# Experts work on gathered tokens in four column groups, with weights loaded by a number found on the chip

## The chip, the cores and the metric

The kernel runs on one core of one Trainium2 chip, alone. The time is device microseconds for one execution. The engines are TensorE (PE; its weight load is PEld), VectorE (DVE), ScalarE (ACT), GpSimd (POOL), and SyncE (SP), whose queue here only issues DMAs. DMAs are issued by SP, ACT and POOL queues.

## The reference, cut to what matters

The model is a stack of twelve layers on x, of 2 batches of 128 tokens of 256 numbers, all in float32. The change is in the third: a mixture of experts with two shared blocks and sixteen routed experts. Each token chooses two experts.

```
shared_out = _gated_mlp(x, shared_w1, shared_w3, shared_w2)      # silu(x @ w1.T) * (x @ w3.T) @ w2.T, 512 wide
gates = softmax(x @ wg.T)                                        # 16 experts
topk_w, topk_idx = top_k(gates, 2);  topk_w /= sum(topk_w)
combine = zeros(T, 16).at[rows, topk_idx].set(topk_w)            # T = 256 tokens
for each expert (w1, w3, w2, cw):                                # 256 wide
    acc = acc + cw[:, None] * _gated_mlp(x, w1, w3, w2)
out = shared_out + acc
```

Ahead of it stand a cross attention on a context of 2 x 2048 tokens and an mLSTM with a gated MLP of four blocks. Behind it comes a causal-style cross attention on the same context (32 units of head and batch).

## The kernel before, in words

Every engine has one program, written out in order; semaphores order the engines among each other. Nothing is planned at run time.

**Gated blocks.** The MLP (blocks 0 to 3), the shared expert (4 and 5) and the sixteen experts (6 to 21) are 22 blocks of one shape: 256 wide up parts w1 and w3, and a down part w2, 768 KB for the three. `Gated.up` (L460) makes eight products of 128 x 128 weights with all 256 tokens; L422 is their line. ACT takes silu of one half (L489), DVE multiplies by the other (L496), `Gated.down` (L470) makes four products (L480), and DVE adds the result to x, for the experts scaled by the token's weight for this expert (L508, L510). So each expert computes all 256 tokens, and the weight is zero for those that didn't choose it. PE issues the up part of block n+1 ahead of the down part of block n. Weights lie in a ring of three slots in the tile `big`; SP loads block n+3 when block n's down part is done (L458). The experts run in a loop of three blocks a turn. The last block's adds are `add_last` (L562), called from the stage behind, which starts with them.

**Router.** `Router.vector` (L788) finds the two largest logits of a token with small DVE operations on 32 columns; it runs beside block 4's up part.

**Around it.** `Split` (L1367) turns the context's keys into three bfloat16 parts, 16 blocks of four POOL operations and a store to DRAM (`key_parts`): six ahead of the mLSTM, ten after block 4's gate. `Mlstm` (L565) needs POOL three times for a root (L152, L153), at the start, in the middle and near the end. `Early` (L1046) computes keys and values for a later layer in 16 pieces, in the gaps of PE; its keys (L1089) are products with 32 stationary columns in four column groups of the array, its values are L1097. SP stores its pieces (L1118). `Causal` (L1463) is the stage behind: SP loads the split keys of unit u in three DMAs (L1422) into one of four slots in the tile `kt`, four units ahead, and one piece of 256 KB of later weights a unit (L1561). PE makes the scores (L1582) and transposed scores (L1593), DVE the maxima (L1716), POOL a shift (L1517), ACT the exponentials (L1663), PE the product with the values in the tile `vv` (L1434). The values were loaded at the start for the first cross attention and stay. POOL's `gpsimd` (L1503) of it begins with a memset of three partitions of `kt` (L1508) and, once the last block is down, a mask (L1510).

## Time and profile before

| | us |
|---|---|
| median of 3 runs | 1100.19 |
| lowest, highest | 1099.86, 1101.62 |
| the profiled execution | 1103.23 |
| its span | 1101.4 |
| gated blocks 4 to 21 in it | 146.3 to 241.8 |

The granted clock of PE was 0.993 over the span. PE ran 9611 products and as many weight loads, of 23433 instructions in all. The core moved 100.39 MB, a mean of 91 GB/s. In the page's 40 slices (27.5 us each) the DMA engines were busiest in the first two (383 and 299 GB/s). A row of a stretch gives busy us of each engine with the number of its operations, the granted clock (1.00 is 2.4 GHz, 0.50 is 1.2 GHz), the DMA engines' busy share and GB/s. In the chain a row is a piece of the work that ended last.

### The profile page before, as it was taken

The page shows a single profiled execution, that of the slowest core. Times are in us where ns is not written, and L with a number is a line of the kernel's source. Part 1 is how long each engine was busy: PE and PEld are TensorE (multiplying, and loading weights), DVE is VectorE, ACT ScalarE, POOL GpSimd, SP SyncE. Part 2 cuts the span into 40 slices and gives each one's busy share as a digit, 9 for nine tenths or more (in the row PEclk, how much of TensorE's full clock was granted, in tenths as well). Part 3 has the DMA queues.
Part 4 walks back from the last instruction along what each step waited for, and adds up shares of the span by engine and source line. Part 5 has one row for each costly group of instructions (what it writes and reads, how often), then busy time and mean ns, then how long its engine had stood idle before and what let it go on. Part 6 is the DMA issues. An engine that isn't in the chain of part 4 may idle for free.

```text
span 1101.4 us, 23433 instructions
## 1 busy us (share of the span) xinstructions
PE 1041.8 (95%) x9611; PEld 845.6 (77%) x9611; DVE 698.0 (63%) x1330; ACT 504.3 (46%) x876; POOL 234.0 (21%) x360
## 2 busy tenths in 40 slices
PE   8999999998999989999988899999999999999886
PEld 3765778875777646677775788999999999999764
DVE  3655243247788368888744876776666577677466
ACT  3242232126677448888855624433342233332384
POOL 4701048402132000000010711110001043332120
PEclk9999999999999999999999999999999999999997
DMA  9712346554673517000141000131111122100000
GB/s 383 299 69 79 133 164 214 191 148 121 184 193 106 178 41 263 2 2 2 40 153 40 1 1 20 33 120 41 39 39 58 40 77 68 59 20 10 1 1 10
DMA packets 37158, 100.39 MB, mean 91 GB/s; under 512 B 4033, under 2 KB 12609, under 8 KB 35393
## 3 DMA queue, kind: packets, MB, share of 16 engines
q1 hardware_dynamic: 33152, 87.35, 24.2%
q0 software_dynamic: 2752, 9.44, 2.5%
q10 hardware_dynamic: 1152, 2.16, 0.5%
q8 instruction: 74, 1.21, 0.5%
q14 instruction: 28, 0.22, 0.1%
HBM read 83.73 MB, written 15.20 MB: 90 GB/s over the span
## 4 chain that ended last, share of the span: by engine, by line
PE 81%; DVE 12%; ACT 3%; issue 2%; DMA 1%; POOL 1%; SPq 0%; DVEq 0%; ACTq 0%; POOLq 0%
PE ps L2276 11%; PE ps L2233 10%; PE ps L422 8%; PE ps L1434 6%; PE ps L1790 6%; PE ps L2131 4%; PE ps L2120 4%; PE ps L480 3%; PE ps L1781 3%; PE ps L1582 3%; PE ps L1593 3%; PE ps L415 3%; PE ps L1097 2%; PE ps L1089 2%; PE ps L291 1%
## 5 line engine op out<-in xcount | busy, mean ns | idle before, releaser
L2276 PE MATMUL ps<-vv,prob 128*128 128x129 f32 x1024 | 126.5, 276 | 1.7 <-DVE xn L2463 1.7
L2276 PEld LDWEIGHTS ps<-vv,prob 128*128 128x128 f32 x1024 | 119.6, 191 | 2.5 <-ACT prob L2382 2.1
L2415 DVE TENSOR_REDUCE probT<-ps 128x128 f32<-128x1024 f32 x64 | 82.5, 1290 | 21.9 <-PE ps L2233 12.9
L1716 DVE TENSOR_REDUCE st<-ps 128x1 f32<-128x512 f32 x128 | 82.4, 686 | 18.0 <-PE ps L1582 16.0
L2382 ACT ACTIVATE prob<-prob 128x1024 f32<-128x1024 f32 x64 | 71.1, 1111 | 27.4 <-DVE prob L2427 27.4
L2355 ACT COPY w<-ps 128x128 f32<-128x128 f32 x32 | 8.5, 266 | 160.0 <-PE ps L2242 160.0
L422 PE MATMUL ps<-xT,big 128*128 128x256 f32 x352 | 79.8, 381 | 0.7 <-ACT xT L707 0.7
L2427 DVE TENSOR_TENSOR prob<-ps,probT 128x1024 f32<-128x1024 f32 x64 | 79.6, 1285 | 1.1
L1663 ACT ACTIVATE prob<-ps 128x1024 f32<-128x1024 f32 x64 | 65.8, 1030 | 28.0 <-PE ps L1593 26.8
L422 PEld LDWEIGHTS ps<-xT,big 128*128 128x128 f32 x352 | 66.2, 190 | 11.2 <-ACT xT L707 0.9
L152 POOL TENSOR_SCALAR small<-small 128x4 f32<-128x4 f32 (+1 forms) x44 | 9.9, 226 | 300.3 <-DVE small L2170 156.3
L2233 PE MATMUL ps<-big,kt 128*128 128x128 f32 x512 | 60.2, 276 | 2.3 <-DVE prob L2427 2.3
L2233 PEld LDWEIGHTS ps<-big,kt 128*128 128x128 f32 x512 | 58.5, 192 | 3.8 <-DVE prob L2427 2.2
L2233 PE MATMUL ps<-w,kt 128*128 128x128 f32 x512 | 60.0, 275 | 0.0
L2233 PEld LDWEIGHTS ps<-w,kt 128*128 128x128 f32 x512 | 58.4, 192 | 0.1
L496 DVE TENSOR_TENSOR prob<-prob,ps 128x512 f32<-128x512 f32 x22 | 15.1, 687 | 67.0 <-ACT prob L489 67.0
L1845 ACT COPY big<-ps 128x512 f32<-128x512 f32 x80 | 45.4, 588 | 20.1 <-PE ps L1790 20.1
L2163 ACT ACTIVATE kt<-ps,w 128x512 f32<-128x512 f32 x32 | 21.8, 690 | 71.4 <-PE ps L2140 71.4
L489 ACT ACTIVATE prob<-ps 128x512 f32<-128x512 f32 x22 | 13.1, 597 | 86.3 <-PE ps L422 86.3
L153 POOL TENSOR_TENSOR small<-small,const 128x4 f32<-128x4 f32 (+1 forms) x44 | 51.0, 1158 | 3.7
L2120 PE MATMUL ps<-qz,big 128*128 128x128 f32 x384 | 47.1, 276 | 0.7 <-ACT kt L2163 0.7
L2131 PE MATMUL ps<-qz,big 128*128 128x128 f32 x384 | 47.0, 275 | 0.0
(476 smaller groups left out, 2282.6 us busy)
## 6 DMA issues: line engine op xcount, KB each, us to landing
big<-blocks_in SPq DMA_DIRECT2D x22, 768.0 KB, 4.3
big<-ctxT_in SPq DMA_DIRECT2D x24, 512.0 KB, 4.1
key_parts<-w POOLq DMA_DIRECT2D x16, 384.0 KB, 4.7
kt<-key_parts SPq DMA_DIRECT2D x32, 192.0 KB, 3.3
vv<-ctx_in SPq DMA_DIRECT2D x2, 2176.0 KB, 24.9
vv<-early_values SPq DMA_DIRECT2D x4, 1088.0 KB, 12.0
kt<-ctxT_in SPq DMA_DIRECT2D x2, 2048.0 KB, 12.4
kt<-key_parts SPq DMA_DIRECT2D x32, 128.0 KB, 3.2
```

The lines of the kernel that those rows point to most:

```text
L422: last = pe.matmul(out, w[:, c, lo:lo + P], xT[:, :, c, :], start=(c == 0), stop=(c == DC - 1))
L1434: last = pe.matmul(self.k.ps[g:g + 17, bank, 0:P], self.values(u, ch), pT[:, ch * P:(ch + 1) * P], start=(ch < 4), stop=(ch + 4 >= MC))
L1663: act.activation(self.pT[:, u % 2, h * 1024:(h + 1) * 1024], k.bank(2 + 2 * h, 1024, 2), ACT.Exp).then_inc(s("exp"), 1)
L1716: dve.tensor_reduce(self.mx[:, u % 2, n:n + 1], k.ps[:, n % 2, :], AX.X, ALU.max).then_inc(s("reduced"), 1)
L1790: last = pe.transpose(k.ps[:, bank, ch * P:(ch + 1) * P], self.p[u % 4][:, (4 * n + ch) * P:(4 * n + ch + 1) * P], k.const("ident"))
L2120: last = pe.matmul(k.ps[:, bank, t * P:(t + 1) * P], tile[:, c, t * P:(t + 1) * P], self.ctx("wk_ctx", DC)[:, c, h * DH:(h + 1) * DH], sta ...
L2131: last = pe.matmul(k.ps[:, bank, t * P:(t + 1) * P], tile[:, c, t * P:(t + 1) * P], self.ctx("wv_ctx", DC)[:, c, h * DH:(h + 1) * DH], sta ...
L2233: last = pe.matmul(k.ps[:, ch // 4, ch % 4 * P:ch % 4 * P + P], keys[:, ch * P:(ch + 1) * P], q, start=True, stop=True)
L2276: last = pe.matmul(k.ps[:, 7, 0:DH + 1], self.prob(u)[:, ch * P:ch * P + P], v, start=(ch == 0), stop=(ch == MC))
L2382: act.activation(e, e, ACT.Exp).then_inc(s("c3_exp"), 1)
L2415: dve.tensor_reduce(self.largest[:, h * P:(h + 1) * P], bank.rearrange("p (c t) -> p t c", t=P), AX.X, ALU.max).then_inc(s("c3_max"), 1)
L2427: dve.tensor_tensor(self.prob(u)[:, lo:hi].rearrange("p (c t) -> p c t", t=P), k.bank(0, hi, 5)[:, lo:hi].rearrange("p (c t) -> p c t", t= ...
```

## The change

Each expert now computes only tokens that chose it. The 512 choices (256 tokens, two each) get places in 32 blocks of 32 slots. Blocks 0 to 15 are the first 32 choices of expert 0 to 15. What an expert has above 32 goes to further blocks, 16 to 31, which are given out in order of the experts. A round works on four blocks at once, one in each column group; there are 8 rounds. The weights of blocks 0 to 15 are loaded by number into sixteen homes. After round t's up and down parts, its homes are loaded with the weights of blocks 16 + 4t to 19 + 4t: SP reads the expert's number from SBUF into a register and issues a DMA at a computed address, once for the up parts (512 KB) and once for the down part (256 KB).

- PE: `ranks` counts choices ahead of a token with products of triangular and all-ones matrices; `rows` turns eight columns (places and weights) into rows; `gather` multiplies the normalized tokens by a one-hot matrix (256 tokens by 128 slots), so that each column group has its 32 tokens as stationary columns; `up` streams 512 columns of w1 and w3 through them; `turn` transposes the gated result; `down` streams 256 columns; `combine` multiplies by a weighted one-hot matrix and accumulates in the two PSUM banks that already hold the shared experts' sum. x is added to once, at the end.
- DVE: `tables` and `places` (16 small operations) and, per round, `make_pick`, `gate`, `make_give`. ACT: per round four operations of 256 columns.
- The four MLP blocks and the two shared ones stay as they were, with a ring at another place of `big`. The tiles w03, kt, vv, big, prob and qz become parts of one arena, so that homes lie in any of them. Expert 0 to 3 take most of `vv`, whose values are loaded again for the stage behind, in four DMAs of 1.04 MB.
- POOL: the split blocks move: 6 to 14 stand between the mLSTM's first and second root, 15 between the second and third. The memset of `kt` is cut in two; its second half runs when the experts are done.
- SP: experts 0 to 9 are loaded ahead of the MLP, 10 to 15 during blocks 3 to 5, the found ones in the rounds. Keys of units 0 and 1 are loaded ahead of the found weights, those of 2 and 3 behind the last combine.

The semaphores of the mLSTM are renamed (m_ to l0_) and used on. The diff, cut to its core:

```diff
+HOMES = [begin("vv") + MC * VH * q for q in range(4)] + [begin("w03"), begin("qz") + 512]
+HOMES += [begin("big") + EXP * i for i in range(3)] + [begin("kt") + 2048]
+HOMES += [begin("big") + EXP * i for i in (5, 3, 4, 6, 7)] + [begin("prob")]
...
+    LOADED = (80, 80, 48, 96, 96, 64)       # Gated.up(n) waits for block_in{n % 3}
...
+class Experts:
+    def load_found(self, sp, dram, t, lo, n, sem):
+        for g in range(4):
+            i = 4 * t + g
+            e = sp.value_load(self.found[0:1, i:i + 1], min_val=0, max_val=EXPERTS - 1)
+            at = HOMES[i] + lo
+            sp.dma_start(self.k.arena[:, at:at + n], dram[bass.ds(e, 1)].rearrange("a p n -> (a p) n")[:, lo:lo + n]).then_inc(self.k.s(sem), 16)
+    def found_sync(self, sp, dram):
+        sp.wait_ge(s("l0_hin"), 4)
+        for t in range(5):
+            if t < 4:
+                sp.wait_ge(s("block_up"), 6 + t + 1)
+                if t >= 2:
+                    sp.wait_ge(*((s("w0_in"), 96) if t % 2 else (s("block_in1"), 160)))
+                self.load_found(sp, dram, t, 0, 1024, "w0_in" if t % 2 else "block_in1")
+            if t >= 1:
+                sp.wait_ge(s("block_y"), 6 + t)
+                if t >= 2:
+                    sp.wait_ge(s("block_in2"), 64 + 64 * (t - 1))
+                self.load_found(sp, dram, t - 1, 1024, 512, "block_in2")
+    def early_sync(self, sp, dram, moe, early):
+        ...                                  # stores 0, 1
+        sp.wait_ge(s("c_product"), 8)
+        for e in range(4):
+            self.load(sp, dram, e, "block_in0")
+        early.store(sp, 2)
+        sp.wait_ge(s("l0_proj"), 3)
+        self.load(sp, dram, 4, "block_in1")
+        for n in range(3, 10):
+            early.store(sp, n)
+        sp.wait_ge(s("l0_hin"), 2)
+        ...                                  # experts 5 to 7 (block_in1), 8 and 9 (block_in2), store 10, tables
+    def up(self, pe, t):
+        ...
+        for c in range(DC):
+            for g in range(4):
+                last = pe.matmul(k.ps[32 * g:32 * g + 32, t % 2, :], self.tokens[t % 2][:, c * P + 32 * g:c * P + 32 * g + 32],
+                                 self.weight(t, g, 512 * c, 512), start=(c == 0), stop=(c == 1))
+    def down(self, pe, t):
+        ...                                  # the same with hT and 256 columns, into bank 4
+    def gather(self, pe, t):
+        ...
+        for c in range(DC):
+            for b in range(B):
+                last = pe.matmul(k.ps[:, 2 + t % 2 * 3, c * P:(c + 1) * P], k.xn[:, b, c * P:(c + 1) * P], self.pick[t % 2][:, b * P:(b + 1) * P],
+                                 start=(b == 0), stop=(b == 1))
+    def combine(self, pe, t):
+        ...
+        for b in range(B):
+            last = pe.matmul(k.ps[:, 6 + b, b * D:(b + 1) * D], self.give[t % 2][:, b * P:(b + 1) * P], self.y[t % 2],
+                             start=False, stop=(t == ROUNDS - 1))
+    def tensor(self, pe):
+        gated.up(pe, 4)
+        self.ranks(pe)
+        gated.up(pe, 5)
+        gated.down(pe, 4)
+        gated.down(pe, 5)
+        self.rows(pe)
+        self.gather(pe, 0)
+        self.gather(pe, 1)
+        for t in range(ROUNDS + 3):
+            if t < ROUNDS:
+                self.up(pe, t)
+            if 0 <= t - 2 < ROUNDS:
+                self.down(pe, t - 2)
+            if 0 <= t - 1 < ROUNDS:
+                self.turn(pe, t - 1)
+            if 0 <= t - 3 < ROUNDS:
+                self.combine(pe, t - 3)
+            if t + 2 < ROUNDS:
+                self.gather(pe, t + 2)
+    def vector(self, dve, o, between):
+        self.gated.gate(dve, 4)
+        self.tables(dve, o)
+        self.gated.gate(dve, 5)
+        self.make_pick(dve, o, 0)
+        self.make_pick(dve, o, 1)
+        self.places(dve, o)
+        ...                                  # per round: make_pick(t + 2), gate(t), make_give(t - 1)
...
 class Causal: sync
         for u in range(32):
             if u >= 4:
                 sp.wait_ge(*self.at("keys_queries", 2 * (u - 3)))
+            if u == 2:
+                found_sync()
+                sp.wait_ge(k.s("l0_proj"), 6 + ROUNDS)
             self.load_keys(sp, u)
-            if u == 3:
-                early.stored(sp, early.LATE)
-                sp.wait_ge(k.s("block_y"), 23)
+            if u in (2, 3, 4, 5):
+                self.reload_values(sp, u - 2, ctx)
...
 build: gpsimd
-            Mlstm.gpsimd(k, pool, o)
+            Mlstm.gpsimd(k, pool, o, 0, 1)
+            split.gpsimd(pool, o, split.BEFORE_MLSTM, split.LAST)
+            Mlstm.gpsimd(k, pool, o, 1, 2)
+            split.gpsimd(pool, o, split.LAST, len(split.BLOCKS))
+            Mlstm.gpsimd(k, pool, o, 2, 3)
             Norm.gpsimd(k, pool, o, 2)
-            pool.wait_ge(s("block_h"), 5)
-            split.gpsimd(pool, o, split.BEFORE_MLSTM, len(split.BLOCKS))
```

## Rows read from the trace of the kernel before

**Rows 1.** The page's parts 1 and 4, of the whole span

```profile
PE 1041.8 (95%) x9611; PEld 845.6 (77%) x9611; DVE 698.0 (63%) x1330; ACT 504.3 (46%) x876; POOL 234.0 (21%) x360
...
PE 81%; DVE 12%; ACT 3%; issue 2%; DMA 1%; POOL 1%; SPq 0%; DVEq 0%; ACTq 0%; POOLq 0%
```

**Rows 2.** Stretches: window and us, busy us by engine, granted clock, DMA share, GB/s

```profile
10.00:20.00 10.00, 8.87 (x32) 3.38 (x32) 5.61 (x9) 3.90 (x4) 8.26 (x8) 1.00 1.03 433
...
146.30:241.80 95.50, 95.03 (x438) 81.86 (x438) 32.50 (x79) 20.71 (x28) 46.89 (x52) 1.00 0.57 184
...
258.00:268.00 10.00, 9.78 (x174) 6.98 (x172) 7.99 (x16) 7.57 (x14) 3.38 (x12) 1.00 0.70 198
...
274.00:276.00 2.00, 2.00 (x23) 1.05 (x25) 1.48 (x3) 1.02 (x1) 0.00 (x0) 0.50 0.19 29
```

**Rows 3.** Chain in order of time: start us, us, what

```profile
69.21 1.88 PE ps L742 x16
...
98.24 0.87 PE ps L755 x8
...
140.29 1.85 PE ps L1089 x16
...
145.35 1.06 PE ps L415 x8
146.41 7.00 PE ps L422 x32
153.42 1.73 PE ps L480 x8
155.14 3.45 PE ps L422 x16
...
241.01 0.50 DVE x L562
```

**Rows 4.** Timeline, ACT and DVE: start us, us, engine line op, idle before

```profile
60.99 0.38 ACT L680 COPY attT<-ps 128x256 f32<-128x256 f32 x1 [2.08 <-PE ps L422]
...
85.70 0.42 DVE L641 TENSOR_TENSOR big<-att 128x256 f32<-128x256 f32 x1
...
149.71 0.19 DVE L813 TENSOR_TENSOR small<-small 128x32 f32<-128x32 f32 x1
...
152.05 0.69 DVE L496 TENSOR_TENSOR prob<-prob,ps 128x512 f32<-128x512 f32 x1
```

**Rows 5.** DMA issues, 140 to 245 us: size, median us from issue to landing

```profile
big<-blocks_in SPq DMA_DIRECT2D x16, 768.0 KB, 4.3
...
early_keys<-big ACTq DMA_DIRECT2D x1, 256.0 KB, 2.1
```

**Rows 6.** Timeline of 225 to 275 us, SP's queue

```profile
228.62 0.33 SPq L458 DMA_DIRECT2D big<-blocks_in  x1
229.22 8.22 SPq L1422 DMA_DIRECT2D kt<-key_parts  x12
```

**Rows 7.** Timeline of POOL, around the mLSTM and beside the experts

```profile
54.66 0.69 POOL L153 TENSOR_TENSOR st<-st,const 128x2 f32<-128x2 f32 x1
103.46 0.21 POOL L152 TENSOR_SCALAR small<-small 128x16 f32<-128x16 f32 x1 [48.10 <-DVEq L643]
...
177.13 0.62 POOL L1387 CAST w<-kt 128x512 bf16<-128x512 f32 x1
...
182.01 0.61 POOL L1387 CAST w<-kt 128x512 bf16<-128x512 f32 x1
...
202.04 3.51 POOL L1508 MEMSET kt<- 3x4096 f32 x1
```

**Rows 8.** Timeline of the stage behind the experts: POOL, SP's queue, PE

```profile
250.89 0.19 POOL L1517 CAST probT<-st 128x1 bf16<-128x1 f32 x1 [8.32 <-DVE st L1727]
...
258.65 3.05 SPq L1422 DMA_DIRECT2D kt<-key_parts  x3
...
271.52 0.59 PE L1582 MATMUL ps<-kt,qz 96*128 96x512 bf16 x2 [1.45 <-issue]
```

More of the change, by code:

```diff
@@ L523, in mlp_vector @@
             if n < 4:
-                self.gate(dve, n, n % 3)
+                self.gate(dve, n)
             if n >= 1:
-                self.add(dve, n - 1, (n - 1) % 3)
-    def moe(self, eng, first, second):
-        first(4, 1, 1)
-        with eng.Fori(0, self.TIMES) as i:
-            for j in range(3):
-                n = i * 3 + (4 + j)
-                first(n + 1, (2 + j) % 3, i + (5 + j) // 3)
-                second(n, (1 + j) % 3, i * 3 + j)
-        for n in range(4 + 3 * self.TIMES, self.LAST):
-            if n + 1 < self.LAST:
-                first(n + 1, (n + 1) % 3, (n + 1) // 3)
-            second(n, n % 3, n - 4)
@@ L543, in moe_tensor @@
-    def moe_tensor(self, pe):
-        self.moe(pe, lambda n, r, t: self.up(pe, n, r, t), lambda n, r, m: self.down(pe, n, r))
-    def moe_scalar(self, act):
-        with act.Fori(0, BLOCKS_MOE // 3) as i:
-            for j in range(3):
-                self.silu(act, i * 3 + (4 + j), (1 + j) % 3)
-    def moe_vector(self, dve):
-        cw = self.k.cw
-        def second(n, r, m):
-            if not isinstance(n, int) or n < self.LAST - 1:
-                self.add(dve, n, r, lambda b: cw[:, bass.ds(m + b * BLOCKS_MOE, 1)])
-        self.moe(dve, lambda n, r, t: self.gate(dve, n, r), second)
+                self.add(dve, n - 1)
@@ L661, in vector, with gpsimd @@
             last = dve.scalar_tensor_tensor(t[:, b], k.xn[:, b], k.st[:, 38 + b:39 + b], w("norm2_w"), ALU.mult, ALU.mult)
-        last.then_inc(s("m_hin"), 1)
+        last.then_inc(s("l0_hin"), 1)
     @staticmethod
-    def gpsimd(k, pool, o):
+    def gpsimd(k, pool, o, first, last):
         s = k.s
-        for n in range(3):
+        for n in range(first, last):
             pool.wait_ge(s("sum_squares"), n + 1)
@@ L791, in v @@
             return k.small[:, 160 + 32 * i:192 + 32 * i].rearrange("p (b e) -> p b e", b=B)
-        lg, key, pick, sel, e = v(0), v(1), v(2), v(3), v(4)
+        lg, both, sel, pick, e, key = v(0), v(1), v(2), v(3), v(4), k.small[:, 322:354].rearrange("p (b e) -> p b e", b=B)
         m = k.small[:, 320:322]
@@ L2808, in build @@
         gated = Gated(k)
+        experts = Experts(k, gated)
         scratch = nc.dram_tensor("key_parts", (B * DC, 3, P, M), BF16).ap()
@@ L2840, in _ @@
             sp.dma_start(k.w0.ap, dram["w0"]).then_inc(s("w0_in"), 16)
-            gated.sync(sp, dram["blocks"], early, (k.w2, dram["w2"]))
+            for n in range(3):
+                gated.load(sp, dram["blocks"], n)
+            experts.early_sync(sp, dram["experts"], dram["moe"], early)
+            sp.wait_ge(s("block_y"), 1)
+            gated.load(sp, dram["blocks"], 3)
+            sp.dma_start(k.w2.ap[:, W2_FIRST:], dram["w2"][:, W2_FIRST:]).then_inc(s("w12_in"), 16)
+            for n in (4, 5):
+                sp.wait_ge(s("block_y"), n - 2)
+                gated.load(sp, dram["blocks"], n)
+            experts.late_sync(sp, dram["experts"], early)
             def parts(to, source, n, loaded):
@@ L2882, in _ @@
             early.copied(pe, 11)
-            gated.moe_tensor(pe)
+            experts.tensor(pe)
             n1.tensor(pe)
@@ L2937, in _ @@
             Router.scalar(k, act)
-            gated.moe_scalar(act)
+            experts.scalar(act)
             n1.scalar(act)
@@ L3096, in constants, with expert_tables @@
     return pack(*[np.asarray(p, np.float32) for p in parts])
+def expert_tables():
+    import numpy as np
+    p, e = np.arange(P), np.arange(EXPERTS)
+    parts = [every(p), p[:, None] + P * np.arange(ROUNDS)[None, :], every(P * np.arange(ROUNDS)), every(e[None, :] < e[:, None]),
+             every(SLOTS * np.arange(1, 8)), every(e), every(SLOTS * e - 1.0), every(SLOTS * e - 480.0)]
+    return pack(*[np.asarray(v, np.float32) for v in parts])
 def layouts(a):
```

498 lines of the change are left out of this document (356 added, 142 removed).

## The prediction

> **What bounds the kernel now.** I read the busy shares first [rows 1]: PE works 95% of the span and holds 81% of the chain, so time is won only by taking work off PE or by ending a wait of PE. Then the stretches [rows 2]: from 146.3 to 241.8 us, the gated blocks of the first feed-forward part, PE is busy 95.0 of 95.5 us at the full granted clock, DVE 32.5, ACT 20.7. Then the chain in order of time [rows 3]: from 146.41 to the first add on x at 241.01 it is nothing but PE, one block costing 3.45 (16 records of L422) + 1.73 (8 of L480) = 5.18 us. A float32 product is two records. Of the 18 blocks two are shared and stay; 16 are experts: 16 x 5.18 = 82.9 us, all on the path.
>
> **The new work on PE, priced by rows.** A round has four column groups, one block each. Its up part is 8 products with 32 stationary and 512 moving columns: 16 records of just the form of L1089, which took 1.85 us [rows 3]. That row also shows that four groups really run side by side: L480's 8 records of 256 columns take 1.73, so 16 records of 512 one after another would take 6.9. The down part has half the columns, 0.93. Two transposes of the gated rows: a quarter of L755's 0.87, so 0.22. Combine: 4 records of 256 columns, half of L480's row, 0.86. Gather: 8 records of 128 columns, half of L742's 1.88, so 0.94. Eight rounds of 1.85 + 0.93 + 0.22 + 0.86 = 3.86 are 30.9; six gathers lie inside the rounds (two stand ahead), 5.6. Together 36.5 us. DVE has per round a pick (four 128-wide operations), a gate (0.42) and a give (0.69 + 0.42), some 2.6 us; ACT four copies or activations of 0.38 [rows 4]. Both stay below PE's 4.8 a round and are hidden by it; if they weren't, the round would still be 4.8.
>
> **Ahead of the rounds.** The chain of before starts L422 at 146.41. After: block 4 up, 3.5 us, to 149.9; the rank products (10 short records, priced by L415's 8 in 1.06 [rows 3]) 1.2, to 151.1; block 5 up, to 154.6; down 4, to 156.3. DVE meanwhile ends the router at about 150.9, gates block 4 (0.69), makes the tables: ten operations of 0.23 with their gap and two 256 wide of 0.46 [rows 4], 3.2 us, to about 155.0; gate 5 to 155.8. It is not late, so down 5 ends at 158.0. Then nothing covers PE well: 8 transposes of rows 0.87, two ACT copies of 512 columns (0.6 each), the two gathers (1.9, beside the copies), the copy of tokens 0.38: the first up part starts at about 161.2. Rounds: 161.2 + 36.5 + 1.0 for the copies between the last turn, down and combine that no other round covers = 198.7. By PE alone the first add on x moves from 241.0 to 198.7, 42.3 us.
>
> **The loads of the found experts.** Rounds 4 to 7 use weights whose expert is known only from the counts. SP reads 16 numbers from SBUF into a register, each twice, and issues a DMA after each: 32 reads and 32 issues in a row, the first after up(0), 163.1 (SP is free by then: its six key loads for rows 0 and 1 take 6 x 0.68 = 4.1 us [rows 6] from about 158). An issue with a computed address took 0.33 us (L458) [rows 6]. The bytes are 16 x 768 KB = 12.6 MB, at the 433 GB/s of the stretch 10 to 20 us [rows 2] 29 us: from 163.1 to 192 + 2, ahead of what PE needs. The bound above: 768 KB took 4.3 us to land and 256 KB 2.1 [rows 5], so 512 KB more cost 2.2, 238 GB/s for one transfer at a time, 53 us for all. With four issued in a row I stay near the first, where several were in flight. The register read has no row. From below it is nothing. From above it is what a whole small DMA takes, 2.1 us from issue to landing for 256 KB [rows 5]. I take 0.75: of that 2.1, 0.6 us is data at 433 GB/s, and of the remaining 1.5, which holds a descriptor, a read, a write and its receipt, a bare read is about half. That is an estimate. So 32 x (0.33 + 0.75) = 34.6, issues end at 197.7, the last 256 KB land 2.3 us later (200.0), then down(7) 0.93, copy 0.5, the first combine 0.43: 201.9. This is later than PE's 198.7 and sets the end. I add 2 us for the four places where SP waits for the landing of an earlier group and for matmuls at a lower clock after such waits (the row at 274 us shows 0.50 right after PE had stood 1.45 us [rows 2, 8]): 204. Gain 241.0 - 204 = 37.0.
>
> The Trainium skill ("Runtime: NRT & Kernel Launch", Instruction fetch mechanics and the preamble table) has two figures for a register load: about 200 ns a register, and about 1.3 us for one round trip to HBM for a few words. No row here shows either. By the first, PE's 198.7 would set the end; by the second, as an estimate, the issues alone would last 32 x 1.63 = 52 us and the end would be near 221.
>
> **What moved into the front.** POOL's ten split blocks that ran from 152 on now stand between the root operations of the mLSTM: nine ahead of the second. A block has a period of 4.87 us (177.13 to 182.01), nine are 43.8; POOL stood idle 48.1 us there [rows 7]. The idle time hides them with 4.3 to spare; without it, every us over would be a us of the chain (DVE L647, PE, ACT wait behind it). The one after takes 4.9 of the gap to the third root. I take 0; bounds 0 and +5 (a store that is waited for, as among the first splits). The loads of experts 4 to 9 (4 after the projections, the others at about 110.5) are behind waits of the block products: experts 5 to 7, 2.4 MB, land by about 119, block 1's up part wants them at 121.6; 8 and 9 by 123.5, block 2 wants them at 126.9. Cost 0, up to +2. The late six are 4.7 MB: the last is issued at about 158 and lands by 163; round 2 wants them at 167.
>
> **Behind the stage.** Keys 2 and 3, the memset of 2048 columns (half of 3.51 us [rows 7]) and four reloads of values of 1.04 MB now start when the experts end. Keys 2 are wanted about 10 us later, and the memset ends ahead of POOL's first shift, which came 9.9 us after the end [rows 7, 8]: hidden. The reloads aren't wholly: two go out beside key loads where the engines are 0.70 busy already [rows 2], and that stage has no slack, since PE stood 1.45 us for keys at 270 [rows 8]. One is 2.4 us of all engines at 433 GB/s; the free 0.30 of a 3.2 us step takes 1.0; 1.4 to 1.5 is left, twice: +3. Bounds 0 (the keys pass between) and +8.
> The extra steps on DVE (ranks, columns, places) are inside the stage's start above. The mask on POOL and DVE's preparations now lie earlier, 0.
>
> **Sum.** -37.0 + 0 + 3 = -34. The profiled run took 1103.23 us (span 1101.4), 3.0 over the median of 1100.19; I take the difference as the same: 1100.2 - 34 = 1066. The likeliest case's own range: a read of nothing and no stall behind, -42.3, 1058; a read of 1.0 us (+8) and 5 behind, 1076.
>
> **Rivals.**
> 1. *SP's reads bind, or the bytes do.* Each 0.1 us of a read over 0.75 costs 3.2 us at the end of the stage. For it: they stand in one queue, one after another, and no row prices them; against it: nothing but their being short. Midway between my 0.75 and the 1.8 of the next rival, at 1.3 us, the end is 163.1 + 32 x 1.63 + 4.2 + 2 = 221.5, gain 19.5, minus 3: 1084. At 238 GB/s the bytes alone end at 163.1 + 53 + 4.2 = 220, the same place. The case holds 1076 to 1095. The Trainium skill's second figure (same page) would be this case.
> 2. *The same, so slow that the change loses.* The point is where 163.1 + 32 x (0.33 + r) + 6.2 + 3 passes 241.0, r = 1.8 us. At r = 2.1, the time of a whole small DMA, it is 241 + 6.2 + 3 = 250: slower by 9, 1109. For it: the bound is a real row; against it: a read of four bytes should need less than a transfer with its receipt.
> 3. *The stage behind starves.* The reloads and key loads jam for all of the first eight steps, and PE at the low clock doubles its share: +10 in place of +3, 1073 to 1078. For it: the 1.45 us stand, the clock of 0.50 and the 3.05 us that SP took to issue three key loads there [rows 2, 8]. Against it: keys are issued between reloads.
> 4. *The front is late.* POOL or an expert load holds the mLSTM or block 1: +5, 1071. For it: 4.3 us to spare of 43.8; against it: POOL's period was steady from 152 to 201.
> A case in which the column groups don't overlap is excluded by L1089's row.
>
> **How the numbers follow.** Forecast 0.62; rival 1, 0.17; rival 2, 0.07; rival 3, 0.08; rival 4, 0.06. The predicted time is the forecast's, 1066. The range 1057 to 1088 takes the forecast's own range, rivals 3 and 4 and most of rival 1; rival 2 and the top of rival 1 are left out, about 0.12, and the forecast's ends, 0.06. A measurement of this kernel tells 0.2% (2.2 us) from no change. Faster is all but rival 2 and a sliver of rival 1: 0.92; within 0.2%, 0.01; slower 0.07.
>
> **What would show it.** PE records of the up parts in groups of 16 in 1.85 us from about 161; a round of 4.8 us in rounds 0 to 3. SP's issues of the found loads spaced by 1.1 us show the read; 0.4 to 0.5 would make it 198.7, 1.6 rival 1, 2.4 rival 2. PE idle ahead of up(6), up(7) and down(7) released by DMA shows who binds. POOL's second root still at 103.5 shows the front free. The first add on x near 204 and the stage behind it 3 us longer than before confirm the sum; a first add before 200 or after 213 makes the forecast wrong, and so does a mLSTM that ends over 2 us later.

## The result, and the profile after

The changed kernel takes 1087.36 us (median, 1085.62 to 1089.4) against 1100.16 in the same session; the ratio is 0.988, 95% interval 0.9864 to 0.9897. It is faster, by 12.8 us (1.2%) and not by 34; 1087.36 is at the upper edge of the range of 1057 to 1088. All positions below are us from the start of the span of the profiled execution (1087.6 after, 1101.4 before).

The page's parts 1 and 4, to lay beside [rows 1]:

```profile
PE 1007.3 (93%) x9608; PEld 800.2 (74%) x9608; DVE 706.2 (65%) x1352; ACT 500.8 (46%) x889; POOL 243.3 (22%) x361
...
PE 72%; DVE 15%; issue 4%; ACT 3%; DMA 2%; SPq 2%; POOL 1%; DVEq 0%; POOLq 0%; ACTq 0%
```

PE lost 34.5 us of work, but only 13.8 of span: DVE's share of the chain rose from 12 to 15%, and DMA and SP's queue, which held 1% between them, now hold 4%. Each of those words names one of the places where the gain went. The stretches, columns as in [rows 2] (window and its us, busy us of PE, PEld, DVE, ACT, POOL, granted clock, DMA share, GB/s), are the way to the rounds, rounds 0 to 4, the last rounds, and the first steps of the stage behind:

```profile
154.70:170.40 15.70, 15.70 (x85) 13.69 (x86) 11.75 (x49) 4.53 (x8) 0.56 (x1) 0.89 0.53 179
170.40:190.80 20.40, 19.73 (x185) 10.67 (x184) 10.47 (x30) 6.24 (x17) 0.00 (x0) 1.00 1.03 350
190.80:222.80 32.00, 21.75 (x168) 11.24 (x168) 8.43 (x23) 6.59 (x16) 0.00 (x0) 0.85 0.69 240
222.80:258.00 35.20, 25.37 (x263) 15.37 (x263) 23.31 (x51) 15.17 (x27) 7.18 (x20) 0.94 0.79 224
```

PE is full up to 190.8, as forecast, but for 0.68 us ahead of up(2), which waits for an expert that is loaded during blocks 3 to 5 and that the forecast had in time; in the next 67 us it works 47. PE's timeline after, which answers to the chain of [rows 3] (start, us, what, idle before and what ended it):

```profile
124.84 7.17 PE L440 MATMUL ps<-xT,arena 128*128 128x256 f32 x32 [0.68 <-ACT xT L985]
...
198.82 3.09 PE L620 MATMUL ps<-arena 128*32 128x512 f32 x16 [3.07 <-DMA arena<-experts_in]
...
208.14 1.93 PE L620 MATMUL ps<-arena 128*32 128x512 f32 x16 [3.61 <-DMA arena<-experts_in]
...
217.97 1.93 PE L633 MATMUL ps<-arena 128*32 128x256 f32 x16 [3.57 <-DMA arena<-experts_in]
219.84 3.70 PE L662 MATMUL ps<-attT,arena 128*128 128x256 f32 x8
```

The MLP's first products start at 124.84 where they started at 118.13. Two of the last up parts and the last down part wait over 3 us for a load of a found expert, and what follows two of the three waits runs partly at the low clock: 3.09 us for up(6) and 1.93 for down(7), which take 1.92 and 1.07, and 3.70 for L662's eight, which take 1.99 at full speed. up(7), behind the longest wait, ran at full speed (1.93). SP's queue over the same stretch, and one line of it in detail (line, operation, count, shortest, median and longest ns, first and last start):

```profile
173.66 41.52 SPq L547 DMA_DIRECT2D arena<-experts_in  x32
```

```profile
L545 SPq TENSOR_LOAD <-small x32: 263/268/458, 172.7 to 214.1; - x32
L545 SPq FUSED_REGOPS  x32: 152/152/187, 173.2 to 214.4; - x32
```

Most issues within a group of four are 1.09 to 1.10 us apart, of which the read itself is 0.27; 1.08 was forecast from an issue's 0.33 [rows 6] and the estimate of 0.75 for the read. The burst lasts 41.5 us and not 34.6, because it pauses twice (3.9 us between two issues ahead of the down parts of round 5, 4.35 ahead of those of round 7), each time in `wait_ge` for the landing of an earlier group.

In the front POOL itself was not late (it ended its nine blocks at 104.6 and was asked for the root at 108.28). DVE was: one of its operations beside one of POOL's, two timelines of the changed kernel:

```profile
79.09 1.00 DVE L900 TENSOR_TENSOR small<-small 128x8 f32<-128x8 f32 x1
```

```profile
77.91 2.16 POOL L1667 TENSOR_TENSOR w<-arena,w 128x512 f32<-128x512 f32 x1
```

DVE's 8-column operation, 0.17 us before the change, ends at 80.09 and POOL's at 80.07; POOL's own takes 2.16 in place of 1.16. Each holds up the other. Over the whole front, from the mLSTM's first root to the MLP, DVE was busy 34.76 us before and 40.73 after, with the same 56 operations (columns as above):

```profile
51.48:118.13 66.65, 61.04 (x375) 37.26 (x373) 34.76 (x56) 23.26 (x39) 6.10 (x8) 1.00 0.21 81
```

```profile
52.03:124.84 72.81, 64.13 (x370) 38.41 (x368) 40.73 (x56) 23.44 (x39) 55.07 (x58) 0.95 0.57 203
```

The front has a number of such places (L900 again at 97.68, 1.00; L910 at 102.58, 0.96 in place of 0.17; L859 at 55.95, 2.10 for two in place of 0.88). A further one stands behind the MLP, where the memset of ones now runs beside the norm: DVE, then POOL,

```profile
150.16 2.34 DVE L211 TENSOR_SCALAR xn<-x,st 128x256 f32<-128x256 f32 x2 [1.16 <-POOL st L171]
```

```profile
150.23 1.80 POOL L1787 MEMSET arena<- 3x2048 f32 x1
```

2.34 us for the two in place of 0.73.

### The profile page after: what moved, and what is told of

The parts are those of the page before. It is cut to its first block, busy times and chain, and to the rows that moved or that the text cites. A ratio compares the mean times of both kernels' runs of the same rounds, so it can differ in the third digit from the quotient of the medians.

```text
span 1087.6 us, 23494 instructions
## 1 busy us (share of the span) xinstructions
PE 1007.3 (93%) x9608; PEld 800.2 (74%) x9608; DVE 706.2 (65%) x1352; ACT 500.8 (46%) x889; POOL 243.3 (22%) x361
## 3 DMA queue, kind: packets, MB, share of 16 engines
q10 hardware_dynamic: 1152, 2.16, 0.5%
## 4 chain that ended last, share of the span: by engine, by line
PE 72%; DVE 15%; issue 4%; ACT 3%; DMA 2%; SPq 2%; POOL 1%; DVEq 0%; POOLq 0%; ACTq 0%
PE ps L2569 11%; PE ps L2526 10%; PE ps L1713 6%; PE ps L2083 6%; PE ps L2424 4%; PE ps L2413 4%; PE ps L440 3%; PE ps L2074 3%; PE ps L1871 3%; PE ps L1882 3%; PE ps L433 3%; DMA arena<-experts_in 1%; PE ps L309 1%; PE ps L1721 1%; PE ps L2433 1%
## 5 line engine op out<-in xcount | busy, mean ns | idle before, releaser
L2569 PE MATMUL ps<-arena 128*128 128x129 f32 x1024 | 126.6, 276 | 1.7 <-DVE xn L2756 1.7
L2569 PEld LDWEIGHTS ps<-arena 128*128 128x128 f32 x1024 | 119.6, 191 | 2.5 <-ACT arena L2675 2.1
L2186 DVE CUSTOM_DVE_ANT_0 arena<-ps,arena 128x1024 f32<-128x1024 f32 x64 | 75.8, 1222 | 21.7 <-PE ps L2074 18.4
L2675 ACT ACTIVATE arena<-arena 128x1024 f32<-128x1024 f32 x64 | 71.1, 1111 | 27.4 <-DVE arena L2720 27.4
L1956 ACT ACTIVATE arena<-ps 128x1024 f32<-128x1024 f32 x64 | 65.7, 1029 | 34.7 <-PE ps L1882 33.7
L2720 DVE TENSOR_TENSOR arena<-ps,probT 128x1024 f32<-128x1024 f32 x64 | 79.6, 1286 | 1.1
L2154 ACT ACTIVATE arena<-arena,st 128x1024 f32<-128x1024 f32 x64 | 73.9, 1156 | 0.0
L2083 PE MATMUL ps<-const,arena 128*128 128x128 f32 x512 | 69.9, 279 | 1.6 <-ACT arena L2138 1.6
L1713 PE MATMUL ps<-arena 128*17 128x128 f32 x2048 | 69.2, 276 | 0.0
L2413 PE MATMUL ps<-arena 128*128 128x128 f32 x512 | 62.4, 276 | 0.7 <-ACT arena L2456 0.7
L2424 PE MATMUL ps<-arena 128*128 128x128 f32 x512 | 62.6, 275 | 0.0
L2526 PE MATMUL ps<-arena 128*128 128x128 f32 x512 | 60.2, 276 | 2.3 <-DVE arena L2720 2.3
L2424 PEld LDWEIGHTS ps<-arena 128*128 128x128 f32 x512 | 60.3, 192 | 2.5 <-issue 2.4
L2526 PEld LDWEIGHTS ps<-arena 128*128 128x128 f32 x512 | 58.5, 192 | 3.8 <-DVE arena L2720 2.2
L1713 PEld LDWEIGHTS ps<-arena 128*17 128x17 f32 x2048 | 50.8, 98 | 13.8 <-issue 7.8
L2413 PEld LDWEIGHTS ps<-arena 128*128 128x128 f32 x512 | 59.6, 192 | 1.6 <-ACT arena L2456 1.2
```

The source lines that it names most:

```text
L1713: last = pe.matmul(self.k.ps[g:g + 17, bank, 0:P], self.values(u, ch), pT[:, ch * P:(ch + 1) * P], start=(ch < 4), stop=(ch + 4 >= MC))
L2083: last = pe.transpose(k.ps[:, bank, ch * P:(ch + 1) * P], self.p[u % 4][:, (4 * n + ch) * P:(4 * n + ch + 1) * P], k.const("ident"))
L2154: act.activation(e, e, ACT.Exp, bias=self.nm[:, u % 2:u % 2 + 1]).then_inc(s("exp"), 1)
L2186: dve.tensor_tensor_reduce(out=self.p[u % 4][:, h * 1024:(h + 1) * 1024], in0=k.bank(2 * h, 1024, 2), in1=self.mask[:, u // 16, h * 1024:( ...
L2413: last = pe.matmul(k.ps[:, bank, t * P:(t + 1) * P], tile[:, c, t * P:(t + 1) * P], self.ctx("wk_ctx", DC)[:, c, h * DH:(h + 1) * DH], sta ...
L2424: last = pe.matmul(k.ps[:, bank, t * P:(t + 1) * P], tile[:, c, t * P:(t + 1) * P], self.ctx("wv_ctx", DC)[:, c, h * DH:(h + 1) * DH], sta ...
```

## The experiments

All profiles are of one shape, so four distances tell them apart: the root ahead of the mLSTM to the first MLP product (the front), from there to up(0), from the first MLP product to the first add on x, and from there to the end. Whole times are medians. The three groups of kernels, each with its own runs of the kernel before (medians 1101.15, 1100.96, 1101.77), can be compared by their ratios.

| kernel | front | MLP to up(0) | MLP to add | add to end | whole | ratio, interval |
|---|---|---|---|---|---|---|
| before | 66.65 | | 122.88 | 860.4 | 1100.16 | 1 |
| changed | 72.81 | 45.53 | 97.96 | 864.8 | 1087.36 | 0.988, 0.9864 to 0.9897 |
| f0_again (the same) | 70.64 | 43.96 | 96.16 | 860.6 | 1082.91 | 0.9834, 0.9794 to 0.9873 |
| e1_stale | 66.55 | 43.95 | 96.38 | 863.7 | 1080.83 | 0.9825, 0.98 to 0.985 |
| e2_fixed | 70.80 | 43.95 | 92.94 | 863.6 | 1079.54 | one run |
| e3_half | 71.36 | 45.51 | 91.89 | 865.4 | 1080.78 | one run |
| e4_sems | 72.34 | 47.17 | 91.74 | 863.6 | 1081.12 | 0.9811, 0.9766 to 0.9857 |
| f1_splits | 68.53 | 47.22 | 100.75 | 864.3 | 1089.22 | 0.9881, 0.9842 to 0.992 |
| f2_once | 70.54 | 43.95 | 89.56 | 868.1 | 1080.78 | 0.9805, 0.9751 to 0.9858 |
| f3_spread | 71.98 | 42.35 | 93.61 | 868.7 | 1088.61 | 0.9884, 0.9845 to 0.9923 |
| h1_noreload | 71.63 | 43.96 | 96.91 | 857.3 | 1079.29 | one run |
| h2_pieces | 71.97 | 45.52 | 98.54 | 860.4 | 1080.93 | 0.9809, 0.9784 to 0.9834 |
| g_all | 69.56 | 42.38 | 90.76 | 858.1 | 1070.49 | 0.9714, 0.9691 to 0.9736 |

Executions of one kernel differ by some 9 us over the sessions (the changed one's 1080.6 to 1089.4, the one before's 1097.9 to 1107.3). A verdict on a few us therefore rests on the distance that the edit touches, and the whole time only has to agree.

**Splitting left out (e1_stale).**

```diff
+            if n < self.BEFORE_MLSTM:
                 o.step(pool.tensor_copy(part[:, 0], key))
                 ...
```

> The ten later split blocks keep only their store; their four POOL operations each are left out, so the planes behind them are not computed. Theory A (the front is late because DVE's small operations run slowly beside POOL's tensor operations, not because POOL itself is late): the first product of the MLP moves back from 124.8 us to about 118.7, L900 back from 1.00 to about 0.17 us, and the whole kernel is about 6 us faster than the changed one, near 1081. Rival (the loads of experts 4 to 9, which now run in the front, or a clock that is lower there, are the cause): the first MLP product stays above 122 and the time stays within 2 us of 1087.

Measured: PE's timeline has

```profile
118.28 7.17 PE L440 MATMUL ps<-xT,arena 128*128 128x256 f32 x32 [0.68 <-ACT xT L985]
```

that is 66.55 us of front, what the kernel before has (66.65), and DVE's work in it is back to what it was, as is L900:

```profile
51.73:118.28 66.55, 60.68 (x372) 36.85 (x370) 34.70 (x56) 23.24 (x39) 14.14 (x18) 1.00 0.65 231
```

```profile
76.68 0.17 DVE L900 TENSOR_TENSOR small<-small 128x8 f32<-128x8 f32 x1
```

This holds though the loads of experts 4 to 9 and the stores of the planes still run there. The other eleven profiles of kernels with the splitting in have 68.5 to 72.8, and DVE busy 38.0 to 42.3 us in it. So POOL's arithmetic in the front is the cause of the delay, and these rows say how, through DVE; the rival falls. The whole time doesn't confirm the size: 0.9825 against 0.9834 for the changed kernel in its second session is no difference, against 0.988 in its first it is some 6 us. In the profiles the stretch from the first add on x to the norm behind the keys stage took 3.0 us more in e1_stale than in that second session (138.65, 135.60); its reloads are the same.

**No reads (e2_fixed).**

```diff
-            e = sp.value_load(self.found[0:1, i:i + 1], min_val=0, max_val=EXPERTS - 1)
...
-            sp.dma_start(..., dram[bass.ds(e, 1)].rearrange("a p n -> (a p) n")[:, lo:lo + n])
+            sp.dma_start(..., dram[i][:, lo:lo + n])
```

> The found experts of rounds 4 to 7 are loaded at fixed expert numbers, without a register read ahead of each (so the weights of those rounds are not those that the counts find); the bytes, the order and the waits for earlier groups are the same. Theory B (the bytes bind: 12.6 MB of found weights with the engines 100% busy from 172 to 208 us): issues come 0.35 to 0.7 us apart, the waits for landings grow, and the first add on x stays at 217 or later (222.8 in the changed kernel). Rival C (the reads bind, 32 x 0.75 us of them): the end of the stage comes down to about 208 and the kernel to about 1073.

**Half the bytes (e3_half).** In the same line `[:, at:at + n // 2]` and `[:, lo:lo + n // 2]`.

> The found loads bring only the first half of the columns of each weight (6.3 MB in place of 12.6; the other half of the weights is old data); the 32 reads, 32 issues and the waits stay. Theory B (bytes bind): PE's waits for a DMA ahead of up(6), up(7) and down(7) (3.07, 3.61 and 3.57 us) vanish or fall under 1 us each, and the first add on x comes near 213: the reads and issues alone end near 173.7 + 35 = 208.7, and the last piece, down, copy and combine take some 4 to 5 us more. Kernel near 1078. Rival C (reads bind): the waits stay over 2 us each and the end is above 219.

**A semaphore for each group (e4_sems).**

```diff
-                if t >= 2:
-                    sp.wait_ge(*((s("w0_in"), 96) if t % 2 else (s("block_in1"), 160)))
-                self.load_found(sp, dram, t, 0, 1024, "w0_in" if t % 2 else "block_in1")
+                self.load_found(sp, dram, t, 0, 1024, self.FOUND_UP[t][0])
```

and the same for the down parts, on semaphores that other loads have done with.

> Each group of found loads counts its landing on a semaphore of its own, so SP waits for no earlier group to land before it issues the next (SP lost some 3.9 and 4.35 us so); bytes, reads and order are the same. If the landing waits bind: SP's last issue moves from 214.8 to about 208.7, the first add on x from 222.8 to 214 to 216, the kernel 7 to 8 us faster, near 1080. If the bytes bind (theory B): the issues end earlier, but the landings take longer in turn, first add on x at 219 or later, gain under 3 us. If the gaps between the bursts were idle time for the DMA engines, the mean rate rises over 400 GB/s.

Measured, the three together. SP's burst in each, in that order:

```profile
167.47 38.47 SPq L546 DMA_DIRECT2D arena<-experts_in  x32
```

```profile
171.09 37.89 SPq L547 DMA_DIRECT2D arena<-experts_in  x32
```

```profile
177.17 35.45 SPq L547 DMA_DIRECT2D arena<-experts_in  x32
```

Neither reads nor bytes bind alone. Without reads the burst is still 38.5 us long; with half the bytes it is 37.9, and up(7) still waits 3.67 us, though up(6) no longer waits and down(7) only 1.35; without the landing waits it is 35.45, which is 32 x 1.1, the forecast's own price of the reads and issues (34.6). Each edit takes 3 to 6 us off the distance from the MLP to the first add (96.2 and 98.0 in the two profiles of the changed kernel; 92.9, 91.9, 91.7). For e2_fixed theory B had said a first add at 217 or later and rival C 208; it came at 214.07, and the whole at 1079.5 where C had 1073: neither. For e3_half B had said 213 and every wait under 1 us, C over 219; it came at 213.65, with two waits that B had excluded. (The MLP began 3.7 and 3.1 us earlier in these two than in the changed kernel, so the distances say more.) I had expected the bytes to hold e4_sems at 219 or the waits to free it to 214 to 216; in positions it came to 218.39, but its MLP began 1.8 us later than the changed kernel's, so by the distance it lies between, nearer to the second. The queue, the landing waits and the bytes (391 to 412 GB/s in e4_sems' windows of 5 us between 185 and 205, against the 433 of [rows 2]) are three limits within a few us of each other. The records also tell where the first issue comes from. SP's key loads end at 172.56 us in the changed kernel, 0.27 behind up(0), and the first found issue follows 1.10 later. In every profile with a read ahead of it it does so by 1.08 to 1.11, and in e2_fixed by 0.10.

**The changed kernel again (f0_again).** No edit.

> The changed kernel once more, as it is, so that the kernels sent with it have it on the same chip. Theory A holds that its front moves from run to run, because what DVE loses beside POOL hangs on how their operations fall: the first MLP product should come somewhere between 121 and 127 us (124.84, 121.13, 121.76 and 126.65 in four kernels with this same front), and the time near 1084 to 1088. A front fixed at 124.8 would speak for a steady cause.

Measured: first MLP product at 122.00, front 70.64, whole 1082.91. The front moves from run to run, but here not by what theory A names. DVE was busy 40.47 us in it, nearly what it was in the first profile (40.73); the granted clock was 1.00 in place of 0.95, and PE was busy 60.73 us in place of 64.13. The same products in both, the first profile's above:

```profile
59.50 3.66 PE L440 MATMUL ps<-xT,arena 128*128 128x256 f32 x8 [0.68 <-ACT xT L985]
```

```profile
58.83 1.99 PE L440 MATMUL ps<-xT,arena 128*128 128x256 f32 x8 [0.68 <-ACT xT L985]
```

The clock differs behind the front too (block 4's up part took 3.70 us here, 5.39 in the first profile).

**Splitting moved (f1_splits).**

```diff
-    BEFORE_MLSTM, LAST = 6, 15
+    BEFORE_MLSTM, BEFORE_MLP, BEFORE_ROUNDS = 6, 9, 13
...
+            split.gpsimd(pool, o, split.BEFORE_MLP, split.BEFORE_ROUNDS)
             Norm.gpsimd(k, pool, o, 2)
```

and blocks 13 to 15 behind `pool.wait_ge(k.s("block_up"), 7)`.

> The ten later split blocks are all computed, but at other places: three (6 to 8) after the first root of the mLSTM, four (9 to 12) beside the MLP, where POOL stood idle 26.6 us, three (13 to 15) from round 1 on; SP waits for the last of them ahead of the keys of row 8. Theory A (DVE beside POOL): most of the front's delay goes, first MLP product at 119 to 121, and no new delay in the MLP (DVE has over 2.7 us idle a block there); rounds 0 to 3 stay at 4.85 us. First add on x 3 to 6 us ahead of the changed kernel, which is 1081 to 1084. Rival (the work costs the same wherever it stands, through the queue of DMAs or DVE): no gain in the whole time, the delay is only moved into the rounds: first product at 119 to 121 but first add on x still at 222.

Measured: a miss. The front came down to 68.53, but two rows of it show new costs, DVE's last product of the mLSTM (0.88 before) and PE's block 4:

```profile
119.35 2.02 DVE L939 SCALAR_TENSOR_TENSOR att<-xn,st,arena 128x256 f32<-128x256 f32 x2 [0.95 <-POOL st L171]
```

```profile
152.88 6.70 PE L440 MATMUL ps<-xT,arena 128*128 128x256 f32 x16
```

The first is POOL's first block starting right beside it. The second is the low clock after the norm's wait, which all kernels risk as long as xn takes 2.34 us. Inside the MLP the four blocks cost nothing (25.34 us from its first product to xn, 25.32 in f0_again). In the rounds they did: up(3) stands 12.45 us behind up(0), 10.04 in f0_again. The whole is slower than f0_again, 1089.22 to 1082.91. DVE's operations there ran slowly again beside POOL's, and the next gather waited 0.84 and 1.05 us for them; this one takes 0.61 us for the two without POOL:

```profile
174.18 1.81 DVE L763 SCALAR_TENSOR_TENSOR arena<-arena,small 128x128 f32<-128x128 f32 x2
```

The rival was right in effect, the delay was moved, and more; but the way is theory A's, at a place where DVE has no slack.

**Each number read once (f2_once).** e4_sems, and

```diff
+            if i not in self.numbers:
+                self.numbers[i] = sp.value_load(...)
+            e = self.numbers[i]
```

> Each group of found loads has a semaphore of its own, as in e4_sems, and each of the 16 expert numbers is read into a register once and kept, in place of twice: 16 reads and 32 issues, the same bytes. Reads bound e4_sems (issues 35.45 us long, 1.1 us each): with half of them the issues last about 16 x 1.1 + 16 x 0.4 = 24 us, and then the bytes bind: 12.6 MB at some 400 GB/s are 31.5 us. From the first product of the MLP to the first add on x: 97.96 us in the changed kernel, 91.7 in e4_sems; here 87 to 89 if the bytes are the next bound at 31.5 us; 91 to 92 if the bytes bound e4_sems already; 83 or less if the reads were all.

Measured: burst 28.34 us (24 forecast), MLP to add 89.56, 2.2 less than e4_sems, slightly short of the 87 to 89 expected. The bytes are the last of the three limits: PE still waits 2.75 and 2.12 us ahead of up(6) and up(7), with the DMA engines full at 388 to 404 GB/s from 175 to 205 us.

**Ones later, reloads apart (f3_spread).**

```diff
+        pool.wait_ge(k.s("block_up"), 6)
         o.step(pool.tensor_scalar(self.neg_t, k.const("drop_T"), -BIG, None, ALU.mult))
+        o.step(pool.memset(k.kt[96:99, 0:2048], two_ones))
...
-            if u in (2, 3, 4, 5):
-                self.reload_values(sp, u - 2, ctx)
+            if u in (2, 6, 12, 20):
+                self.reload_values(sp, (2, 6, 12, 20).index(u), ctx)
```

> Two moves on the changed kernel: POOL's memset of 3 x 2048 ones stands behind block 5's up part in place of right beside the second norm, and the four reloads of values (1.04 MB each) go out with the keys of rows 2, 6, 12 and 20 in place of 2, 3, 4 and 5. Theory: xn (L211 x2) back from 2.34 to about 0.73 us and block 4's up part from 5.24 to 3.5 us when the clock no longer falls, so 1.6 to 3.3 us less between the last product of the MLP and up(0); behind the stage PE's waits for keys (0.99, 2.62 and 2.96 us at 243 to 255) fall to one of about 1.5, so 3 to 5 us less after the first add on x. Together 5 to 8 us, near 1080. Rival (the keys wait for something other than the reloads): the 864.8 us from the first add on x to the end stay within 1.

Measured: the first half as expected, xn back to 0.73 us and MLP to up(0) 42.35, 1.6 under the 43.95 that five other profiles share. The second half a miss: from the first add to the end 868.7 us, more than ever (1.7 of it at the kernel's end, see below). PE's timeline has a new wait 9.7 us behind the issue of the third reload (264.78),

```profile
274.51 0.59 PE L1871 MATMUL ps<-arena 96*128 96x512 bf16 x2 [2.60 <-issue]
```

A wait "<-issue" in this stage is one for keys. The second reload has one of 2.47 us, 9.3 behind its issue, the fourth one of 1.34, 9.0 behind. So a whole reload of 1.04 MB ahead of a key row holds up PE at the later steps too.

**No reloads (h1_noreload).** The four reloads of values and PE's wait for them are left out.

> The changed kernel without the four reloads of values (the products of the keys stage take what the experts left there). Theory D (the reloads, 4.2 MB between key loads, are what makes the keys stage longer than before): from the first add on x to the end 864.8 us in the changed kernel falls to 857 to 861, PE's waits in the first 35 us of the stage to one of about 1.5. Rival (it is the late start of the keys of rows 2 and 3, or the memset of the other 2048 ones): stays over 863.

**Reloads in pieces (h2_pieces).**

```diff
...
+            for q, first in ((1, 3), (2, 15), (3, 23)):
+                if first <= u < first + 4:
+                    self.reload_values(sp, q, ctx, u - first, u - first + 1)
+            for to, source, loaded in later[self.LATER_BY[u]:self.LATER_BY[u + 1]]:
```

> The changed kernel with the first reload whole and the other three in four pieces of 261 KB, one beside each key row of 3 to 6, 15 to 18 and 23 to 26, where the later weights step aside. Theory D: a whole reload of 1.04 MB holds up the next keys by more than their slack (2.6 us at 57.6 us into the stage in f3_spread, right behind a reload), a piece does not: no PE wait over 1.5 us after the first 35 us of the stage, and from the first add on x to the end 860 to 862. Rival (bytes are bytes, the stage has none to spare): the waits are only spread, 864 or more.

Measured: without reloads 857.3 us from the first add to the end, and the first product of the norm behind the keys stage comes 131.9 us after the first add (132.1 in the kernel before, 139.4 in the changed one): the reloads are the whole of the stage's excess, as far as one profile shows. In pieces the end is 860.4 us away, and the one wait for keys over 0.9 us is

```profile
250.24 0.59 PE L1877 MATMUL ps<-arena 96*128 96x512 bf16 x2 [1.12 <-issue]
```

Both as theory D has it. The changed kernel had three there, of 0.99, 2.62 and 2.96 us. But its second profile, f0_again, had one, of 2.17 us, and was as short: 135.6 us from the first add to that norm and 860.6 to the end, 135.2 and 860.4 in pieces. With whole reloads at the same steps the other seven profiles took 138.3 to 140.2 us to the norm, with pieces the two took 135.2 and (g_all) 132.9. What pieces are worth is thus 3 us or more against most profiles and nothing against one.

**All of it (g_all).** Semaphores, single reads, ones, pieces, and the splitting as

```diff
-    BEFORE_MLSTM, LAST = 6, 15
+    BEFORE_MLSTM, LAST = 6, 12
...
-            Mlstm.gpsimd(k, pool, o, 1, 2)
+            Mlstm.gpsimd(k, pool, o, 1, 3)
+            pool.wait_ge(s("l0_xT"), 3)
             split.gpsimd(pool, o, split.LAST, len(split.BLOCKS))
-            Mlstm.gpsimd(k, pool, o, 2, 3)
             Norm.gpsimd(k, pool, o, 2)
```

> What the runs so far point to, together, with all work done: six split blocks (6 to 11) after the first root of the mLSTM and four (12 to 15) beside the MLP, behind DVE's last product of the mLSTM (POOL 10 of 26 us idle left); a semaphore for each group of found loads; each expert number read once; the memset of ones behind block 5's up part; the reloads of values 1 to 3 in four pieces each, with the keys of rows 3 to 6, 15 to 18 and 23 to 26, and the later weights moved around them. Terms, from profiles of the single edits against the changed kernel's own 96 to 98 us from the MLP to the first add on x: semaphores and single reads to 89.6 (f2_once), less 1.6 for xn without the memset (f3_spread): 88. Front: from the root at 52 to the MLP 66.65 us before, 70.6 to 72.8 in the changed kernel; here 68.5 to 70. Behind: 861 to 863 from the first add to the end if the pieces help, 864 to 868 if not. Root at 52.0 + 69 + 88 + 862 = 1071 of span, about 1073; 1076 to 1079 if the pieces do not help. Rival (each removed wait is taken up by the next one, the bytes): above 1080.

Measured: 1070.49 us (1067.55 to 1071.46), ratio 0.9714 (0.9691 to 0.9736), faster than both kernels. Its terms: front 69.56, MLP to add 90.76 (88 expected), add to end 858.1 (861 to 863 expected). Its chain and the row that is left of the loads:

```profile
PE 75%; DVE 13%; issue 3%; ACT 3%; SPq 2%; DMA 2%; POOL 1%; POOLq 0%; DVEq 0%; ACTq 0%
```

```profile
167.11 30.45 SPq L549 DMA_DIRECT2D arena<-experts_in  x32
...
201.20 2.51 PE L620 MATMUL ps<-arena 128*32 128x512 f32 x16 [3.85 <-DMA arena<-experts_in]
```

The granted clock over the span is 0.997 (0.986 in the changed kernel's profile), so the fewer waits of PE seem worth more than their length. What each of its five edits is worth inside it was not measured one by one.

## Why the prediction was wrong

**Right: PE's work.** PE is full from 154.7 to 190.8 but for the 0.68 us ahead of up(2), the up part's 16 records take 1.92 us (1.85 forecast from [rows 3]), the down part's 1.05 to 1.07 (0.93), the gather 1.05 to 1.06 (0.94), and the steady round 4.85 (4.8): 181.15, 186.00, 190.84 for up(3) to up(5). The column groups overlap. **Right: the read.** 1.09 to 1.10 us an issue with its read, 1.08 forecast, though its row was only bounded by 0 and 2.1. The load alone is 0.27, and with the register operations, the assertion and their gaps around it 0.76. That this met the 0.75 is luck in part: the estimate was for a bare read, cut out of a DMA's 2.1 us, and the rest it didn't count. The Trainium skill has two figures, for loads from HBM, in "Runtime: NRT & Kernel Launch": about 0.2 us a register (Instruction fetch mechanics) and about 1.3 for a round trip (the preamble table and its note). For this number, which lies in SBUF, the first is the near one to the load's 0.27. The mechanism of the forecast, SP's burst of reads setting the end, and its direction were right; its sizes weren't. The first add on x was forecast for 204 (203.9 by its terms) and came at 222.80. Both signs that the prediction had named for being wrong showed: a first add after 213, and an mLSTM that ends over 2 us later. The 18.9 us, term by term, in this profile:

- **"I take 0; bounds 0 and +5" for the front: 6.7** (0.55 of it is the start, 51.48 to 52.03). This is the largest single term here. The step asked whether POOL's idle time holds nine blocks, which it did, and priced being late; it never asked what POOL's tensor operations do to DVE's, which are on the chain there. The rows beside it could have told: in [rows 7] the blocks ran beside expert blocks in which DVE had slack, so a steady period of POOL's was no evidence for DVE. e1_stale shows the cause; the low clock that follows (0.95 over the front) makes it larger than in f0_again.
- **Ahead of the rounds, 43.1 from the MLP to up(0): 45.5, 2.5 more.** 1.6 is the memset beside the norm, which held up xn (f3_spread takes it back); the prediction priced only its other half. 1.7 is the low clock in block 4's up part (5.39 for 3.70). The rest of the way was 0.8 shorter than forecast.
- **The first found issue 1.9 after up(0): 3.3, 1.4 more.** "SP is free by then" was wrong by 0.27 us of key loads, and the first read with its register operations stands ahead of the first issue (1.10).
- **"I add 2 us" for landing waits and low clock: 6.9 in the burst alone, 4.9 more.** e4_sems takes the waits out and the burst is 35.45. The cause is the step that took the landings to be short because "several were in flight": with several under way at once 512 KB took a median of 7.2 us to land, more than the 4.3 that 768 KB took when they came singly [rows 5]. With half the bytes (e3_half) most landed in 2 to 3.5.
- **4.2 from the last issue to the add: 7.6, 3.4 more.** The last landing took 2.8 us (2.3 forecast), then down(7) and the combines at the low clock: 1.93 and 3.70 for 1.07 and 1.99.

6.7 + 2.5 + 1.4 + 4.9 + 3.4 = 18.9. In f0_again, the same kernel, the first add came at 218.16, 14.3 late, and the same five terms are 3.9, 0.9, 1.7, 4.3 and 3.5. So the terms of the found loads (the last three) together outweigh the front in both.

**The stage behind: +3 forecast, +4.4 measured, and near only by accident.** To the norm behind the keys stage it is 139.4 - 132.1 = +7.3 us, near the forecast's bound of +8 and its rival 3: three waits of PE for keys and the low clock after them, all from the reloads (h1_noreload). The six other profiles with the same reloads have +6.2 to +8.1, f0_again alone +3.5. So the forecast's two waits of 1.4 to 1.5 us were too small a price. The other -2.9 come from the last 20 us of the kernel. One row of the kernel before and the one that answers to it after:

```profile
1083.95 3.60 PE L2793 MATMUL ps<-attT,big 128*128 128x128 bf16 x32 [0.47 <-ACT attT L2762]
```

```profile
1072.75 1.96 PE L3086 MATMUL ps<-attT,arena 128*128 128x128 bf16 x32 [0.46 <-ACT attT L3055]
```

The first ran at the low clock, the second didn't. f2_once, a kernel with the change, had 727.9 us behind that norm again, with the same PE waits there as the kernel before (1.63 and 1.30 us at 722 and 724 behind the norm), eight others had 725.0 to 725.4, e3_half 725.8 and f3_spread 727.1: it comes and goes with no part of the change.

Rivals 1, 3 and 4 each happened in part: the landing waits and bytes (rival 1's second half), the starved keys, the late front. I gave them chances as if only one could, and took the likeliest case's sum with each at or near its friendly end. Together, -37 + 18.8 + 4.4 (in place of -37 + 3) is -13.8 of span, and -12.8 between the medians.

**Still open.** The front's loss differs by over 2 us between kernels with the same front (70.54 to 72.81). DVE's own part differs (39.8 to 42.3 us busy), and so does the granted clock (0.95 to 1.00). Why the clock fell in one and not in another, behind waits of the same kind, is not shown. Nor is it shown why the rate of the found loads' first 4 us was 201 to 216 GB/s with the engines busy: the key rows in flight then are the suspect, and they weren't tried elsewhere.

## What to carry to other kernels

Before moving work into an idle stretch of POOL, look at what DVE does there: if its small operations are on the chain, every one of POOL's tensor operations may cost one of them up to its own length. Price a burst of loads with a pace for each of the queue, the semaphores and the bytes; where the three are close, taking one away gives only the distance to the next, and the worth shows when all are taken together. And when several rivals are each likely to happen a little, add them: the sum of their small ends is the forecast, not zero.

## What the runs showed of the hardware

- DVE beside POOL: an 8-column operation 1.00 us in place of 0.17, ending with POOL's TENSOR_TENSOR to 0.02 us; POOL's own 2.16 in place of 1.16; two TENSOR_SCALARs on 256 columns 2.34 in place of 0.73 beside a memset of three partitions by 2048.
- A number of SBUF into a register of SP: 0.27 us for the load, 0.76 with what goes with it.
- After a wait of PE of 2 to 4 us the next groups may run at the low clock, in part or whole (g_all's up(7) after 3.85 us: 2.51 in place of 1.92; L662 x8 3.70 in place of 1.99), but not each time (the changed kernel's up(7) after 3.61 us: 1.93).
- DMAs of 256 and 512 KB in a row: 391 to 412 GB/s with the engines full (e4_sems, 185 to 205 us).
